# Reordering the work of one turn on three engines in a gated-scan and expert-routing kernel

## The reference

```python
mod = (silu(c) @ wmod).reshape(32, 6, 1, 128)          # sa, ca, ga, sb, cb, gb
ga, gb = sign(ga) * max(|ga|, 0.25), sign(gb) * max(|gb|, 0.25)
h = layernorm(x) * (1 + ca) + sa
g, a, v = sigmoid(h @ Wg + bg), sigmoid(h @ Wd + bd), h @ Wv + bv
x = x + ga * (scan(s_t = a_t * s_{t-1} + (1 - a_t) * v_t) * g)
h = layernorm(x) * (1 + cb) + sb
probs = softmax(h @ gate_w.T + gate_b)                  # 8 experts, the best two are kept
y_e = relu(h @ w1[e] + b1[e]) @ w2[e] + b2[e]           # 128 -> 512 -> 128
x = x + gb * sum over the two kept experts of probs[e] * y_e
```

## Time and profile before

| | |
|---|---|
| three executions, us | 541.35 (median), 546.0, 538.31 |
| profiled execution, us | 545.22 |
| its span, us | 543.4 |
| busy, us | PE 424.1, DVE 448.6, ACT 308.7, POOL 210.1 |
| last scatter of the first phase lands, us from the start | 230.5 |
| first matmul of the second phase, us from the start | 234.6 |
| mean granted TensorE clock | 0.878 |

### The profile page before, as it was taken

The page is one execution under the profiler, slowest core; times in us unless marked ns, Lnnn a source line. Parts: engine busy times, 40 slices in busy tenths (PEclk is TensorE's granted clock), DMA queues, the critical chain, the costliest instruction groups (busy, mean ns, idle before and its releaser), DMA issues.

```text
span 543.4 us, 14857 instructions
## 1 busy us (share of the span) xinstructions
PE 424.1 (78%) x4290; PEld 348.0 (64%) x4291; DVE 448.6 (83%) x1242; ACT 308.7 (57%) x777; POOL 210.1 (39%) x279
## 2 busy tenths in 40 slices
PE   2837898784875861069999999999999999999970
PEld 2423655552643751049988998898897888888860
DVE  5799869854798868369999999999999888989960
ACT  1427989773866430046666666656665555556630
POOL 5003322237667357702433443344334433333331
PEclk9868889786979555569999999999999999999985
DMA  8413444114233224231332233223323322222210
GB/s 240 117 39 123 154 140 141 68 46 180 100 117 147 90 99 153 102 88 38 97 94 76 76 99 87 73 77 96 88 79 77 87 80 73 76 67 75 64 37 0
DMA packets 46567, 51.01 MB, mean 94 GB/s; under 512 B 5422, under 2 KB 39679, under 8 KB 46514
## 3 DMA queue, kind: packets, MB, share of 16 engines
q1 hardware_dynamic: 38400, 33.17, 22.1%
q0 software_dynamic: 7040, 16.93, 8.4%
q10 hardware_dynamic: 1074, 0.23, 0.2%
HBM read 27.43 MB, written 24.70 MB: 96 GB/s over the span
## 4 chain that ended last, share of the span: by engine, by line
PE 40%; issue 19%; DVE 19%; POOL 13%; ACT 3%; DMA 2%; SPq 1%; POOLq 0%; DVEq 0%; ACTq 0%
POOL sorted_rows L521 12%; PE bank L1241 5%; PE bank L1257 5%; PE bank L1258 5%; PE bank L1260 5%; PE bank L1243 5%; PE bank L1242 5%; DVE xs L1038 4%; PE bank L1121 4%; DVE st L763 2%; PE bank L1253 2%; DVE hT L1051 2%; PE bank L1227 2%; DVE xn L809 1%; DVE a L1056 1%
## 5 line engine op out<-in xcount | busy, mean ns | idle before, releaser
L542 POOL DMA_INDIRECT out_dram<-tg,midx x92 | 106.7, 1159 | 198.7 <-DVE tg L1059 184.7
L705 ACT ACTIVATE xs<-bank,bcols 128x256 f32<-128x256 f32 x368 | 139.4, 489 | 32.4 <-PE bank L1243 32.0
L1257 PE MATMUL bank<-w2hi,xs 128*128 x736 | 122.7, 220 | 0.0
L1258 PE MATMUL bank<-w2hi,w2f 128*128 x736 | 122.6, 220 | 0.0
L1040 DVE TENSOR_TENSOR w2f<-xs 128x1024 f16<-128x1024 f32 x92 | 112.7, 1225 | 3.2
L1260 PE MATMUL bank<-w2lo,xs 128*128 x736 | 101.7, 220 | 0.0
L1241 PE MATMUL bank<-xh,w1hi 128*128 128x256 f16 x368 | 101.4, 276 | 0.3 <-ACT xs L705 0.3
L1242 PE MATMUL bank<-xl,w1hi 128*128 128x256 f16 x368 | 101.3, 275 | 0.0
L1243 PE MATMUL bank<-xh,w1lo 128*128 128x256 f16 x368 | 101.2, 275 | 0.0
L521 POOL DMA_INDIRECT sorted_rows<-pay,idx x64 | 68.0, 1062 | 34.5 <-issue 18.9
L1258 PEld LDWEIGHTS bank<-w2hi,w2f 128*128 128x128 f16 x736 | 72.5, 99 | 0.0
(11 more groups left out here) (221 smaller groups left out, 706.4 us busy)
## 6 DMA issues: line engine op xcount, KB each, us to landing
xs<-sorted_rows SPq DMA_DIRECT2D x46, 260.0 KB, 2.8
xs<-sorted_rows SPq DMA_DIRECT2D x47, 128.0 KB, 2.5
sorted_rows<-padt SPq DMA_DIRECT2D x10, 582.0 KB, 5.2
w2f<-in_L_ffn_w_dram SPq DMA_DIRECT2D x4, 512.0 KB, 3.8
xs<-in_L_ffn_w_dram SPq DMA_DIRECT2D x4, 512.0 KB, 4.0
out_dram<-tg,midx POOLq DMA_INDIRECT x92, 3.1
xs<-in_L_attn_x_dram SPq DMA_DIRECT2D x2, 512.0 KB, 7.5
sorted_rows<-pay,idx POOLq DMA_INDIRECT x64, 2.7
```

The lines of the kernel that those rows point to most:

```text
L542: pool.indirect_dma_start(out_rows, bass.IndirectOffsetOnAxis(midx[k][:, t:t + 1], 0), yout[k][:, t, :], None, bounds_check=TOK - 1, oob_i ...
L705: ins = act.activation(hf[e][:, cc, :], bank[2 * e + cc // 2][:, (cc % 2) * TW:(cc % 2 + 1) * TW], ACT.Relu, bias=bcols[n % 2][:, e * HC + ...
L1257: pe.matmul(o[t], hh[n % 2][e][:, cc, t * P:(t + 1) * P], whi, start=False, stop=False)
L1258: pe.matmul(o[t], hl[n % 2][e][:, cc, t * P:(t + 1) * P], whi, start=False, stop=False)
```

## The change

DVE: in a turn, residual and the variances now come before choose, pair_rows and place_rows (except pair_rows(3) in turn 15, which stays ahead of residual(15)); in turn 0, normalize(3) comes after residual(0). PE: turn_r(g) comes right behind project(g+1), ahead of the two other groups of transposes; spread_gb(g) is written at the end of turn g and not at the start of turn g+1. ACT: copy_gb(g) comes behind payload, ahead of w_high. The super groups are 3, 4, 3, 2, 2, 2 groups; the first is chosen, paired and placed in turns 6, 7, 8 and the second in 10, 11, 11. Batch 2 leaves `QUICK`. The statistics of groups 1 and 3 are taken between the dependent steps of the first two batches. The first two groups of x are loaded by themselves, the first ahead of wmod.

```diff
-SGS = (4, 4, 2, 2, 2, 2)
+SGS = (3, 4, 3, 2, 2, 2)
-X_CHUNKS = ((0, 1), (2, 3, 4, 5), (6, 7, 8, 9), (10, 11, 12, 13), (14, 15))
+X_CHUNKS = ((0,), (1,), (2, 3), (4, 5), (6, 7, 8, 9), (10, 11, 12, 13), (14, 15))
-QUICK = (0, 1, 2) + tuple(range(len(BATCHES) - 4, len(BATCHES)))
+QUICK = (0, 1) + tuple(range(len(BATCHES) - 4, len(BATCHES)))
-CHOOSE_IN = {7: 0, 11: 1, 13: 2, 14: 3}
-PAIR_IN = {8: 0, 12: 1, 13: 2, 15: 3}
-PLACE_IN = {9: 0, 12: 1, 14: 2}
+CHOOSE_IN = {6: 0, 10: 1, 13: 2, 14: 3}
+PAIR_IN = {7: 0, 11: 1, 13: 2, 15: 3}
+PLACE_IN = {8: 0, 11: 1, 14: 2}
@@ SP
             sp.dma_start(csb[:], c).then_inc(csb_in, 16)
+            load_x_chunk(0)
             sp.dma_start(wmods[:], wmod).then_inc(wmod_in, 16)
-            for c_ in range(len(X_CHUNKS)):
+            for c_ in range(1, len(X_CHUNKS)):
@@ ACT, a turn
-                if turn >= 1:
-                    copy_gb(turn - 1)
...
                 for g in MOD2_IN[turn]:
                     payload(g)
+                copy_gb(turn)
@@ DVE
-            def variances(n):
+            def variances(n, meanwhile=None):
+                rows = [] if meanwhile is None else list(range(meanwhile * GT, (meanwhile + 1) * GT))
+                def step(ins):
+                    mark(ins)
+                    count = steps
+                    if rows:
+                        t = rows.pop(0)
+                        mark(dve.bn_stats(st[:, t, :], xrow(t)))
+                    dve.wait_ge(dve_step, count)
...
-            variances(0)
+            dve.wait_ge(x_in[1], 16)
+            variances(0, meanwhile=1)
...
-            stats1(1, 2)
+            stats1(2)
...
-            variances(1)
+            variances(1, meanwhile=3)
@@ DVE, a turn
                 scan(g)
                 if g == 0:
-                    stats1(3, 4, 5)
+                    stats1(4, 5)
                     variances(2)
-                if g + 3 < NG:
+                if 0 < g < NG - 3:
                     normalize(g + 3)
...
                 if g + AHEAD < NG:
                     stats1(g + AHEAD)
+                if g == NG - 1:
+                    pair_rows(NSG - 3)
+                residual(g)
+                if g == 0:
+                    normalize(3)
+                for n, (end, _, _) in enumerate(BATCHES):
+                    if end == g > 0:
+                        variances(n)
                 if g in CHOOSE_IN and g < NG - 2:
                     choose(CHOOSE_IN[g])
-                if g in PAIR_IN:
+                if g in PAIR_IN and g < NG - 1:
                     pair_rows(PAIR_IN[g])
                 if g in PLACE_IN:
                     place_rows(PLACE_IN[g])
-                residual(g)
-                for n, (end, _, _) in enumerate(BATCHES):
-                    if end == g > 0:
-                        variances(n)
@@ PE, a turn
-                if turn == 1:
-                    pe.wait_ge(setup_dve, DVE_GBROW)
-                    pe.wait_ge(iota_done, 1)
-                if turn >= 1:
-                    spread_gb(turn - 1)
                 if turn + 1 < NG:
                     project(turn + 1)
+                turn_r(turn)
+                if turn in PLACE_IN and turn not in PAIR_IN:
+                    rank_rows(PLACE_IN[turn])
                 for g in MOD2_IN[turn]:
                     turn_xn2(g)
                 if turn + 2 < NG:
                     turn_xn(turn + 2)
-                turn_r(turn)
-                if turn in PLACE_IN and turn not in PAIR_IN:
-                    rank_rows(PLACE_IN[turn])
                 for g in MOD2_IN[turn]:
                     logits(g)
                     turn_back(g)
+                if turn == 0:
+                    pe.wait_ge(setup_dve, DVE_GBROW)
+                    pe.wait_ge(iota_done, 1)
+                spread_gb(turn)
```

More of the change, by code:

```diff
@@ L49 @@
     (g, (), (g,)) for g in range(NG - 4, NG))
-QUICK = (0, 1, 2) + tuple(range(len(BATCHES) - 4, len(BATCHES)))
-CHOOSE_IN = {7: 0, 11: 1, 13: 2, 14: 3}
-PAIR_IN = {8: 0, 12: 1, 13: 2, 15: 3}
-PLACE_IN = {9: 0, 12: 1, 14: 2}
+QUICK = (0, 1) + tuple(range(len(BATCHES) - 4, len(BATCHES)))
+CHOOSE_IN = {6: 0, 10: 1, 13: 2, 14: 3}
+PAIR_IN = {7: 0, 11: 1, 13: 2, 15: 3}
+PLACE_IN = {8: 0, 12: 1, 14: 2}
 NORM2_IN = [()] * 2 + [(g,) for g in range(NG - 5)] + [(NG - 5, NG - 4), (NG - 3,), (NG - 2,), (NG - 1,), ()]
@@ L686, in _ @@
             normalize2(NG - 1)
-            copy_gb(NG - 1)
             modulate2(NG - 1)
@@ L1207, in _ @@
             rank_rows(NSG - 3)
-            spread_gb(NG - 1)
             turn_xn2(NG - 1)
```

## The result

| | before | after |
|---|---|---|
| median, us (20 executions each) | 543.4 (538.31 to 546.68) | 537.51 (535.32 to 538.72) |
| ratio, 95% interval | | 0.9906 [0.9882, 0.993] |
| profiled execution, its span, us | 545.22, 543.4 | 535.87, 534.0 |
| u(11), start of choose(3)'s first reading, idx(3) ready, us | 130.35, 176.93, 194.06 | 114.18, 165.11, 185.05 |
| start of the last scatter, us | 227.67 | 218.16 |

By the medians the change brings 5.9 us, less than half of the 12.3 that were forecast. The second phase is the same to 0.1 us (308.8 us from its first matmul to the end before, 308.9 after), so all of it lies in the first phase. The ratios on record are taken otherwise and come out up to some half a per cent nearer to 1 (537.51/543.4 is 0.989), so the two are not mixed.

The account below looks back on a forecast made before the run. First phase ends a fixed 36.4 us after idx(3); before it ACT sets the pace, with routing DVE. Gain 15.1 - 2.8 = 12.3 us: 545.22 to 532.9 profiled, 0.7% over the median; from the median 529.0 us, range 519 to 538.

Parts of the forecast that it names:

- Step 1: Start, up to the first scan: halved first chunk and moved statistics bring u(0) 0.8 us earlier, at 22.7; bounds 0 and 1.6.
- Step 2: Turn 0: DVE is spared a Newton chain but waits some 2 us for POOL; 0.8 us stays, u(1) at 34.9.
- Step 3: Turns 3 to 10: ACT takes 8.05 us a turn, the ring wait goes, u(11) at 115.4, 15 us earlier.
- It is not late: Ring slot for residual(13): idx(1) comes at the end of turn 11, leaving 11 us against the 7.8 needed.
- up to 5 us: Price put on residual(13) waiting for the ring, in case the scatters of group 3 were late.
- Step 4: Turns 11 to 14: DVE bounds, 46.6 us from u(11) to choose(3)'s reading, at 162.0; gain so far 15.1 us.
- some 1 us: Turns 13 and 14: DVE's wait for turn_r between scan and residual, each time; bounds 0.7 and 1.4.
- Step 5: Tail on PE, choose(3)'s reading to idx(3): turn_r(15), spread_gb(15) and copy_gb(15) add 2.8 us; gain left 12.3 us.
- C: Ring wait returns as another, DVE and PE holding one another in turns 7 to 9; gain 4 to 8 us; 19%.
- B: ACT's turns go at 7.55 us and two clock drops don't occur; gain 17 to 21, 520 to 524 us; 25%.
- D: Slower: PE waits at turn_r in each turn and falls to the lower clock, turns about 12 us; 553 us; 5%.

Follow-up runs that it names:

- place11_again: The changed kernel with place_rows(1) in turn 11 in place of turn 12; 534.87 us, 0.9809 of the kernel before.
- gs_three: Kernel before with the changed kernel's super groups, turns, loads and batches, but place_rows(1) in turn 11 and w1's low halves in eight pieces; 528.44 us, 0.9747.
- tail15: The changed kernel with turn_r(15) behind turn_xn2(13), and spread_gb(15) and copy_gb(15) behind rank_rows(3) and the last normalize2; 546.16 us, 0.9713.
- three: The changed kernel with place_rows(1) in turn 11, turn_r(15), spread_gb(15) and copy_gb(15) later, and w1's low halves in eight pieces; 530.87 us, 0.979.
- sets 3 and 5: Two groups of follow-up runs, each on one chip; the unchanged kernel before took 546.15 us and 545.26 us in them.
- after_again: The changed kernel itself, run again unaltered on a chip of the slower kind; 548.27 us, 0.9738 of the kernel before.
- after_fourth: The changed kernel itself, run again unaltered on another chip of the slower kind; 548.97 us, 0.9787 of the kernel before.

## Why the prediction was wrong

**Step 1, start: wrong in size, within its bounds.** u(0) came at 23.39 and not 22.7, 0.1 us earlier than before and not 0.8. variances(0) did start about when I said (7.06 us, said 6.9). But u(0) waits for ACT [2.60 <-ACT a L604 above], and ACT does gates(0) behind modulate(1), which needs turn_xn(1), which stands behind project(0) on PE. That one began 0.4 us earlier (14.18 against 14.58) and took 5.49 us against 4.84, so it ended later than before. I followed DVE only. The load of x that I had weighed is not what counts here: the first one lands 3.8 us after its issue in the changed kernel (256 KB) and 5.1 us in the kernel before (512 KB). The formula that the prediction took from the Trainium skill, page DMA: Bandwidth & Descriptors, section Anatomy of one DMA, stands there for DMAs that GpSimd issues, and SP issues these loads. It gives by estimate 2.6 and 3.2 us, 0.6 apart; the traces show 1.3 apart and both longer, with other loads ahead in the same queue (c, and in the kernel before wmod too), and they decide.

**Step 2, turn 0: better than said.** u(1) 34.1 (said 34.9), u(2) 43.0 (43.8), u(3) 49.0 (50.0). normalize(3) waited for POOL, but 0.66 us and not 2.

**Step 3, turns 3 to 10: right, but for the ring.** gates(4) started at 51.1 (said 51.9), gates(9) at 90.6 (92.2), gates(11) at 109.0 (110), u(11) at 114.18 (115.4). The pace of ACT is (90.60 - 51.07) / 5 = 7.9 us a turn (said 8.05). "It is not late", of residual(13), failed: I had idx(1) at the end of turn 11, since I had misread the turn. It comes at the end of turn 12, 137.06 us. The price in case it was late, "up to 5 us", was the right one: 4.50. A check was to be had from my own numbers: POOL needs 7.8 us from idx(1) to the landing, and 137.2 + 7.8 is 145. And among the waits before the change I had left out the second longest, 4.33 us of residual(5) for PE behind the stretch at the lower clock:

```profile
75.01 0.69 DVE L831 TENSOR_TENSOR pay<-bank,xs 128x512 f32<-128x512 f32 x1 [4.33 <-PE bank L1127]
```

In the changed kernel residual(5) waits 0.93 us.

**Step 4, turns 11 to 14: the step of the sum that failed.** I had 46.6 us from u(11) to choose(3)'s reading, made of 42.6 of work and 4.0 of waits; 177.15 and 162.0 in the prediction are the end of that instruction. Measured to the same point it was 51.1. The waits of residual in turns 11 to 14 are 1.89, 0.77, 4.50 and 1.51, together 8.7 us; the remaining 42.5 are the work with its short gaps, as said. So the miss is 4.7 us of waits, the term of the sum that failed; 3.5 of it is the wait of turn 13, which I had at some 1 us. choose(3)'s reading ended at 165.32 (said 162.0). Reading the turn rightly would not have saved the step: in place11_again, which is the kernel that I described, it ends at 165.46, since 3.90 us of wait for PE stand behind the ring wait. I had priced that wait at "some 1 us", with project at the higher clock; at the lower one it is 5.15 us and turn_r stands behind it. In gs_three, with routing ahead of residual(13) and project(14) at the higher clock, the reading ends at 162.83 us.

**Step 5, the tail on PE: right in the sum.** From the end of choose(3)'s first reading to idx(3) it is 19.7 us (said 19.7; 16.9 before). The two added pieces stand in PE's timeline of the changed kernel where they were put:

```profile
170.19 1.09 PE L1142 MATMUL bank<-ident,r 128*128 128x128 f32 x4 [0.78 <-ACT pay L636]
...
176.00 1.22 PE L1150 MATMUL bank<-modr,ident 32*128 32x128 f32 x4
```

and tail15, which takes them out, is 2.1 us faster, though its interval overlaps that of the changed kernel; in three the shorter tail brings 1.3 us between these two points. idx(3) came at 185.05, 9.0 us earlier than before, and not 12.3.

**Steps and sum.** By the trace, idx(3) gains 9.0 and the slow scatter 0.5, so 9.4 us between the two profiled executions against 12.3. The rest of the miss is not in the steps. I took the profiled execution of before to be 3.9 us above its usual time; over 20 executions it is 1.8 above, and the profiled one of after is 1.6 below its own median. So of the 8.5 us between 529.0 and 537.51, 3.0 are the steps and 5.5 are the relation of one execution to the many.

Where in an execution these few us vary, I did not find, but they go with the mean granted clock. On the two chips of the faster kind in sets 3 and 5, the 13 executions of the kernel before at 0.884 or above took 537.59 to 544.08 us, and the 20 at 0.879 or below took 544.90 to 546.93. The profiled execution of before, at 0.878, thus belongs with the longer ones, and the profiled one of after had the highest clock of its 20 (0.877 to 0.889).

**The rivals.** C has the time, but only half of the mechanism: the wait went and came back as another, with a gain of 4 to 8 us (5.9; 537.5 against its upper end of 537). I gave it 19%, and looked for it in turns 7 to 9; there the waits of residual are 0.9 us at most, and it was in turn 13. That its number fits is in part luck. B did not come: ACT's pace was 7.9 us and not 7.55. D has nothing for it: the mean clock of the profiled executions did not fall (0.878 and 0.889; the median over the 20 of after is 0.88), and no turn before turn 11 became 12 us. But its mechanism, PE at the lower clock in front of turn_r, is real in one turn, and is the second half of what happened. The Trainium skill, page TensorE: Matmul & The Clock Gate, section Part 1: The HAM clock gate, says that idling lowers the clock; the trace agrees in direction: in place11_again PE stood for 1.92 us for r(12), and the 134 to 144 us behind that are at 0.52. But the length of the last gap does not tell it. D put the gap before 66.4 us at about 2 us; PE's timeline has it at 1.15 us, and the stretch from 73.3 to 100.6 us, with gaps of up to 1.46 us, keeps 1.00. Nor is that stretch the one that shows a busy PE at the lower level; the row above it is, with PE busy for all of 6.90 us at 0.51.

## What to carry to other kernels

When a wait on a ring or a pool of buffers is removed, compute for every later reuse when its slot comes free, from the turn in which the numbers are really written and from what the issuing engine still does ahead of it, and read what second wait stands just behind the first: here 4.50 us were followed by 3.90 of another kind, so the repair was worth 2.0 us by the medians. Work on an engine that looks as if it delayed a chain may be the cover of that chain's round trip over another engine; move it only if the round trip has nothing to wait for. Before gains are added, ask whether two of them fill the same wait. And the rate of a full queue is worth a look at its outlier: the one slow scatter that both profiles showed was the cheapest 3.7 us in this kernel.

## What the runs showed of the hardware that was not expected

**A long DVE instruction holds up the issue of an indirect DMA on POOL.** Under a tensor_tensor of 128x4096 (fp32 in, fp16 out, 4.43 us) one scatter takes 4.69 to 5.20 us and not 0.96, in all five traces in which the two overlap, and each time it ends 0.84 us behind the end of the DVE instruction. In the ten traces in which that instruction comes behind the start of the last scatter, no scatter is longer than 1.50 us. Under four pieces of 128x512 (2.49 us together) the scatter takes 1.36 or 1.44. Splitting and moving it took the long scatter away and brought 3.7 us. What each of the two brought, the cut or the new place, was not taken apart.

**The gain depends on the chip.** The kernel before takes 543 to 546 us in three sets (the result, 3 and 5) and 561 to 564 in the three others, and the changed kernel 0.986 and 0.991 of it on the first kind of chip and 0.974 and 0.979 on the second; the intervals of the two nearest (0.9855 and 0.9787) still touch. On the second kind the traces have waits without a named end, while POOL issues scatters, as this one of ACT in after_again:

```profile
161.32 0.60 ACT L636 ACTIVATE pay<-bank 128x512 f32<-128x512 f32 x1 [6.46 <-remote]
```

and idx(4) follows idx(3) by 11.7 us and not 8.1. There are seven such rows up to 240 us in that trace and six in after_fourth; the eight traces of the first kind have none. The kernel before was not traced on a chip of the second kind, so what the waits are, and whether the change shortens them, stays open.
